# Row fetches by SyncE alone, and index lists read in place, in the gather rounds of a graph network

## What is computed

```python
def _round(x, w, b, gamma, beta, src, dst, etype):
    h = jax.nn.relu(_bn(x, gamma, beta))
    h = jnp.einsum('nd,od->no', h, w) + b
    msg = h.reshape(N, T, D)[src, etype]
    return jax.ops.segment_sum(msg, dst, num_segments=N)
# x = layernorm(x + round2(round1(x)) + x)
# then: h = x @ W_in; W_ij = (ssp(f_ij @ Wf1 + bf1) @ Wf2 + bf2) * cutoff
# out = segment_sum(h[src] * W_ij, dst); x = layernorm(x + ssp(out @ Wo1 + bo1) @ Wo2 + bo2)
```

## Time and profile before

| | |
|---|---|
| median of 3 runs | 8460.24 us (8458.51 to 8467.58) |
| the profiled execution, first to last instruction | 8446.8 us |
| TensorE's mean granted clock in it | 0.707 of full speed |
| TensorE matmul busy | 4102.0 us (49%) |
| DVE busy | 3975.2 us (47%) |
| ACT busy | 1426.6 us (17%) |
| Pool busy | 4532.3 us (54%) |
| first and last start of a table gather, round 0 | 212.9 and 2778.1 us |
| the same, round 1 | 2959.0 and 5539.9 us |
| table gathers in both rounds | 2886 |
| first row fetch of SP in round 0 | 234.0 us |

### The profile page before, as it was taken

The page is one execution under the profiler, slowest core; times in us unless marked ns, Lnnn a source line. Parts: engine busy times, 40 slices in busy tenths (PEclk is TensorE's granted clock), DMA queues, the critical chain, the costliest instruction groups (busy, mean ns, idle before and its releaser), DMA issues. The chain is left out here.

```text
span 8446.8 us, 99538 instructions
## 1 busy us (share of the span) xinstructions
PE 4102.0 (49%) x22648; PEld 3353.5 (40%) x22648; DVE 3975.2 (47%) x7789; ACT 1426.6 (17%) x3513; POOL 4532.3 (54%) x4709
## 2 busy tenths in 40 slices
PE   7342232331023734322232104466667888888888
PEld 3232222221022423222222103345555776777777
DVE  4553333331023567555555205643333555555568
ACT  3000000000000200000000000034444444444423
POOL 4665555564056566555555306656666555555533
PEclk8666666665566766666666556776777899888989
DMA  7111111111012511111111102222223555555567
GB/s 268 46 45 41 42 42 43 42 43 30 7 46 58 190 48 44 42 42 42 43 41 41 27 11 77 79 88 91 93 91 121 171 172 171 170 169 169 171 218 233
DMA packets 467009, 761.62 MB, mean 90 GB/s; under 512 B 115518, under 2 KB 227712, under 8 KB 465698
## 3 DMA queue, kind: packets, MB, share of 16 engines
q1 hardware_dynamic: 310212, 436.97, 17.1%
q0 software_dynamic: 148032, 316.34, 13.1%
q10 hardware_dynamic: 8192, 2.11, 0.1%
HBM read 542.21 MB, written 212.75 MB: 89 GB/s over the span
## 5 line engine op out<-in xcount | busy, mean ns | idle before, releaser
L667 POOL DMA_INDIRECT edge_rows<-messages,idx_stage x1432 | 1368.4, 956 | 1059.3 <-DVE idx_stage L1043 648.2
L1756 PE MATMUL banks<-w_types,h_stage 128*128 128x512 f32 x320 | 321.5, 1107 | 1864.1 <-issue 1153.5
L667 POOL DMA_INDIRECT buf_a<-messages,idx_stage x727 | 695.7, 957 | 715.8 <-DVE idx_stage L1043 487.8
L728 POOL DMA_INDIRECT sorted_rows<-edge_rows,idx_stage x784 | 760.4, 970 | 543.3 <-DVE edge_rows L1576 329.8
L728 POOL DMA_INDIRECT sorted_rows<-buf_a,idx_stage x784 | 760.2, 970 | 538.4 <-DVE buf_a L1576 305.0
L667 POOL DMA_INDIRECT buf_x<-messages,idx_stage x727 | 696.5, 958 | 647.5 <-DVE idx_stage L1043 418.8
L1951 PE MATMUL banks<-work,buf_a 128*128 128x128 f32 x5640 | 839.6, 312 | 144.3 <-issue 98.7
L1951 PEld LDWEIGHTS banks<-work,buf_a 128*128 128x128 f32 x5640 | 798.1, 225 | 196.9 <-issue 187.2
L1756 PEld LDWEIGHTS banks<-w_types,h_stage 128*128 128x128 f32 x320 | 77.1, 299 | 1901.5 <-issue 1175.4
L1998 PE MATMUL banks<-wf,work 128*128 128x128 f32 x3136 | 616.1, 333 | 188.3 <-issue 180.3
L1998 PEld LDWEIGHTS banks<-wf,work 128*128 128x128 f32 x3136 | 487.9, 226 | 363.2 <-issue 362.5
(11 more groups left out here) (222 smaller groups left out, 7592.6 us busy)
## 6 DMA issues: line engine op xcount, KB each, us to landing
buf_a<-sorted_rows SPq DMA_DIRECT2D x705, 288.0 KB
messages<-work SPq DMA_DIRECT2D x196, 320.0 KB
buf_a<-dst_rows SPq DMA_DIRECT2D x198, 256.0 KB
first_batch<-messages SPq DMA_DIRECT2D x2048, 0.5 KB
buf_x<-messages ACTq DMA_DIRECT2D x2048, 0.5 KB
buf_x<-messages SPq DMA_DIRECT2D x2048, 0.5 KB
buf_a<-messages ACTq DMA_DIRECT2D x2048, 0.5 KB
buf_a<-messages SPq DMA_DIRECT2D x2048, 0.5 KB
```

Of the source, the lines that this page charges most:

```text
L667: nc.gpsimd.indirect_dma_start(gathered[p][h][:, t, :], None, source, bass.IndirectOffsetOnAxis(ap=idx_stage[:, h, t:t + 1], axis=0),).the ...
L728: nc.gpsimd.indirect_dma_start(sorted_rows, bass.IndirectOffsetOnAxis(ap=idx_stage[:, 2 * u + h, t:t + 1], axis=0), msg_halves[2 * u + h][ ...
L1756: nc.tensor.matmul(ps_raw[:, 0:WIDE], h_stage[:, t % 2, :], w_types[p][:, 0:WIDE], start=True, stop=True)
```

## The change

The groups that are fetched row by row go from ten to six (three batches, 24 tiles a round instead of 40), and SP issues all of them, each batch whole, in `fetch_batches`; nothing is fetched late, and ACT fetches nothing. `idx_stage`, `s_idx` and `stage_indices` are gone: Pool gives its DMAs the columns of `msg_idx` (in the convolution of `places`) themselves. In the gather pass Pool waits for `s_agg`, TensorE's sums of the half four earlier. Before the second memset it waits for `msg_idx`. TensorE waits for the one-hot matrix once a half instead of once a group. The wide path is reordered.

```diff
-FETCHED = ((112, 0), (114, 0), (132, 0), (134, 0), (148, 0), (150, 0), (176, 0), (178, 0), (184, 0), (186, 0))
+FETCHED = ((112, 0), (114, 0), (148, 0), (150, 0), (184, 0), (186, 0))
 BATCHES = len(FETCHED) // 2
-SP_BATCHES, ACT_BATCHES = (0, 2, 4), (1, 3)
-FETCH_HALF = (None, 2, 3, 5, 6)
-ACT_FIRST_RAW, ACT_UNITS = RAW_TWICE, 4
-LATE_FIRST, LATE_UNITS = {4: 80, 3: 104}, 3
+FETCH_HALF = (None, 3, 6)
...
             def fetch_batches(p):
                 sp.wait_ge(s_setup, FETCH_LINKS)
-                for i in SP_BATCHES:
+                for i in range(BATCHES):
                     if i:
                         sp.wait_ge(s_raw_agg, raw_summed(p, i))
                     if p:
                         sp.wait_ge(s_acc[0], SUMS + 2 * (FETCHED[2 * i + 1][0] - 2 * RAW_ITERS[0] + 1))
-                    for e in late_units(i, 0) if i in LATE_FIRST else range(P):
-                        fetch_rows(nc.sync, mybir.EngineType.SP, p, i, e)
+                    for e in range(P):
+                        fetch_rows(p, i, e)
...
                     fetch_batches(0)
                     for m in range(CHUNKS):
                         store_nodes(TURNED + m, m, y_row_stage)
-                        fetch_late(0, m + 1)
...
                 load_x(m + 1)
-                fetch_late(1, m)
                 store_chunk(m)
...
                 for half in range(2 * RAW_ITERS[p], 2 * ITERS):
                     h = half % GATHER_SLOTS
-                    pool.wait_ge(s_idx[p], half + (1 - 2 * RAW_ITERS[p]))
+                    if half >= 2 * RAW_ITERS[p] + GATHER_SLOTS:
+                        pool.wait_ge(s_agg[p], half + (1 - 2 * RAW_ITERS[p] - GATHER_SLOTS))
...
                             gathered[p][h][:, t, :], None, source,
-                            bass.IndirectOffsetOnAxis(ap=idx_stage[:, h, t:t + 1], axis=0),
+                            bass.IndirectOffsetOnAxis(ap=msg_idx[:, half * HALF_TILES + t:half * HALF_TILES + t + 1], axis=0),
...
             gather_raw(0)
+            pool.wait_ge(s_setup, RANGE_LINKS + 2)
             nc.gpsimd.memset(buf_a[:, 6 * WIDE:NBUF], 0.0).then_inc(s_clear, 1)
...
                 for h in range(2):
-                    pool.wait_ge(s_idx[2], r * 2 + (h + 1))
                     pool.wait_ge(s_tagged, r * 2 + (h + 1))
...
-                                sorted_rows, bass.IndirectOffsetOnAxis(ap=idx_stage[:, 2 * u + h, t:t + 1], axis=0),
+                                sorted_rows, bass.IndirectOffsetOnAxis(ap=places[:, column:column + 1], axis=0),
...
-                    if t >= ACT_FIRST_RAW:
-                        fetch_some(rnd, ACT_UNITS)
-                fetch_some(rnd, P + LATE_FIRST[ACT_BATCHES[-1]] - (RAW_TILES - ACT_FIRST_RAW) * ACT_UNITS)
...
-                    fetch_some(0, LATE_UNITS)
...
                 deviation(m)
-                fetch_some(1, LATE_UNITS)
...
-                stage_indices(p, k + GATHER_SLOTS, 2 * u + h)
...
-                    stage_indices(2, k, 2 * u + h)
```

More of the change, by code:

```diff
@@ L22 @@
-import itertools
 import numpy as np
@@ L389, in raw_summed, with fetch_rows @@
             return RAW_BEFORE[p] // HALF_TILES + FETCH_HALF[i] + 2
[L391 to L395, removed]
+        def fetch_rows(p, i, e):
             rows = table[p].rearrange("(o n) d -> o (n d)", o=1).bitcast(u8)
             at = nc.values_load_multi_w_load_instructions(
-                fetch_at[e:e + 1, i, :, :].rearrange("p j t -> p (j t)"), engines=[kind], min_val=0,
+                fetch_at[e:e + 1, i, :, :].rearrange("p j t -> p (j t)"), engines=[mybir.EngineType.SP], min_val=0,
                 max_val=(N * T - 1) * ROW_BYTES, skip_runtime_bounds_check_because="a source times the types plus a type, in bytes")[1]
@@ L401, in fetch_rows @@
             for t in range(HALF_TILES):
-                engine.dma_start(into[:, t * ROW_BYTES:(t + 1) * ROW_BYTES], rows[:, ds(at[t], ROW_BYTES)]
+                nc.sync.dma_start(into[:, t * ROW_BYTES:(t + 1) * ROW_BYTES], rows[:, ds(at[t], ROW_BYTES)]
                                  ).then_inc(s_fetched[i], 16)
@@ L1795, in aggregate, with rows_in @@
                 rows_in_slot = gathered[p][slot]
-                hot, rows_of = hots[h if beyond else slot], []
+                hot = hots[h if beyond else slot]
+                def rows_in(j):
+                    if j and closing:
+                        return rows_in_slot[:, GROUP_TILES:HALF_TILES, :]
+                    if isinstance(r2, int) and (r * 2 + h, j) in FETCHED:
+                        batch, part = divmod(FETCHED.index((r * 2 + h, j)), 2)
+                        pe.wait_ge(s_fetched[batch], (p + 1) * FETCH_INC)
+                        return fetched[p][batch].rearrange("p (t n) -> p t n", n=P)[
+                            :, part * GROUP_TILES:(part + 1) * GROUP_TILES, :]
+                    pe.wait_ge(s_gather[slot][j], gathers(p, slot, j, r2, r2 if passed is None else passed))
+                    return rows_in_slot[:, j * GROUP_TILES:(j + 1) * GROUP_TILES, :]
+                if beyond:
+                    sum_beyond(p, rows_in, r * 2 + h)
                 for j in range(2):
@@ L1800, in aggregate @@
                     if j and closing:
-                        rows_of.append(rows_in_slot[:, GROUP_TILES:HALF_TILES, :])
                         continue
[L1803 to L1813, removed]
+                    rows_in_group = rows_in(j)
                     if j == 0:
-                        pe.wait_ge(s_acc[p], g + (2, 6)[p])
+                        pe.wait_ge(s_onehot[p], r2 * 4 + (2 * u + h + 1 - 2 * RAW_ITERS[p]))
+                        pe.wait_ge(s_acc[p], r2 * 8 + (4 * u + 2 * h - 4 * RAW_ITERS[p] + (2, 6)[p]))
                     tiles = LAST_TILES if closing else GROUP_TILES
@@ L1961, in beyond_block @@
                     tile = slice(t * P, (t + 1) * P)
-                    last = nc.tensor.matmul(ps_h[j][:, tile], x_onehot[:, 0, tile], x_h, start=opening, stop=False)
+                    last = nc.tensor.matmul(ps_h[j][:, tile], x_onehot[:, 0, tile], x_h, start=False, stop=False)
                 last.then_inc(s_xagg[2], 1)
@@ L1977, in convolution_step @@
                         if beyond:
[L1978 to L1980 removed]
+                            nc.tensor.matmul(ps_h[j], ones_d[0:1, :], zero_col[0:1, :].broadcast_to([1, WIDE]), start=True, stop=False)
+                            with pe.Fori(0, BLOCKS) as b:
+                                beyond_block(k, j, b)
                         for t in range(GROUP_TILES):
@@ L1984, in convolution_step @@
                             last = nc.tensor.matmul(ps_h[j][:, tile], spread[:, h, edges], h_win[:, h, j, :],
-                                                    start=not beyond, stop=True)
+                                                    start=not beyond, stop=not beyond or t == GROUP_TILES - 1)
                         last.then_inc(s_hexp, 1)
```

39 lines of the change are left out of this document (10 added, 29 removed).

## The result

The changed kernel takes 8695.84 us (median of 4 runs, 8676.12 to 8711.81) against 8463.91 us (4 runs) for the kernel before: 232 us slower, and by the runs' means 1.0267 times as long (95% interval 1.0242 to 1.0292). The forecast was 8800. The profiled execution's span is 8674.3 us, 227.5 us above the one before, so the profile holds nearly the whole difference.

What follows compares the result with a forecast made beforehand. SP's row fetches bound each round, at half 148 and at the first stores or loads behind them. Terms 30 + 328 - 20 = +338 us on the 8446.8 span, plus 13.4, gave 8798, say 8800; range 8610 to 8990.

Steps and rivals of the forecast that it cites:

- (b): Third batch: 384 more rows ahead of the first stores (round 0) or `load_x(1)` (round 1), 164 us each, +328 us.
- (a): Gather rounds until half 148's fetched rows: longer streams (gapless Pool gathers) slow SP's rows, +15 a round, +30 us (bounds -16, +254).
- (c): Tails, each round's end behind the fetches: eight more gathers, shorter Pool pauses, together about -20 us (bounds +20 and -132).
- (d): Start: memset waits for msg_idx, first gather some 7 us later; Pool's 70 us wait before half 152 covers it, 0.
- (e): ACT issues 4,096 rows less; raw tiles end ahead of SP's wait at half 148; worth counted in (a), one-hot wait 0.
- (f): Gathers reading the index lists in place: same 955 ns each, 0.
- (g): Third phase: 196 index copies of 165 ns leave DVE, no Pool scatter wait is on them: 0 (bound -32).
- Streams run together: Rival (22%): Pool's gather streams grow to four halves or more, SP falls to 1.8 us a row; 8964 us.
- Faster: Rival (9%): ACT's rows slow SP's; alone SP keeps 0.427 us a row beside Pool, nothing waits for batch three; 7594 us.
- The block is hidden: Rival (4%): first store or load behind the third batch is needed later than read, (b) is 0; 8470 us.

Runs made afterwards that it cites:

- late_back: Changed kernel, but 48 of the last batch's 128 partitions fetched behind the stores and loads, as before: 0.9867 of the kernel before, 8351 us on 8464.
- one_batch_2: Changed kernel with only the first batch (groups 112 and 114) fetched, other groups gathered by Pool, in a slow set: 7515.32 us, 0.8873 of the kernel before.
- before_again: The kernel before, unchanged, run again for its profile, in a quick set: 6277.59 us (one run).

## Why the prediction was right, and where it was off

**What bounds the kernel** was read rightly: SP's rows, twice a round. The strongest evidence is that taking the third batch away, and then the second, made the kernel 643 and then, in another set, 954 us faster than the one before, while Pool did more. In a quick set the same kernel before is not bound by SP.

**(b), the block:** +328 forecast; +158.4 and +162.8 in the profile, 321.2 together, 0.418 us a row against the 0.427 used. late_back gives the same from the other side (0.040).

**(a), up to half 148:** forecast +30, measured -43.1 and -22.8, -65.9, beyond the bound of -16 that I gave it. This is the main miss, and it has three steps. I let streams lengthen once ACT was out (+15 a round). They did not (from 19.9 to 19.6 us in the mean between 700 and 1400 us, though 3 of the 30 came to 30 us). The pauses fell from 5.9 to 2.9 us, more than the 0.8 us a pause which I gave to the copy, since ACT's rows had held TensorE. And I charged each microsecond of pause that goes with a row per 0.427 us; counted by start, a row in a pause took 0.63 us in the kernel before and 0.78 in the changed one. By the same reading too few rows of the 198.5 us were left for the streams, so that 1.28 us a row beside a stream was too slow: over round 0's streams up to half 148 it was 1.03 before and 1.00 after. In the kernel before the two errors cancel (2026 for 2034.3), so that it could not show them; with fewer pauses they do not. Short pauses were worth less to SP than I thought, and streams more. That the total still lay in my range is due to (b), which is the larger term and was right. Pool came to half 152 at 1832.6 and stood 174.2 us, in which SP ran at its full pace.

**(c), the tails:** forecast -20; -13.8 and -14.9, -28.7. **(d), the start:** forecast 0 with cover; the memset's wait moved the first gather by 10.3 us and SP's first row from 234.0 to 241.8, and as SP is the bound its own later start has no cover. I named Pool's waiting as the cover and overlooked that SP waits at the same table: the step failed by some 8 to 10 us. **(e), ACT:** "what that is worth is in (a)" had the wrong sign there, as shown. **(f)** held, 955 ns. That the copies do not slow the gathers held too, though the median in the earlier trace rows could not show it: 176 gathers of the kernel before ran beside a copy and took 954 ns in the mean, the others 957. **(g):** forecast 0, measured -7.2. In sum -65.9 + 321.2 - 28.7 + 10.3 - 7.2 - 2.2 = 227.5 against the 338 forecast; 96 of the 110 us between them are (a)'s.

**The signs named:** the third batch ran from 2002.7 to 2483.0 (said: 2050 to 2530), the pauses were 406.4 at half 159 (380) and 428.8 at half 154 (430), the short ones 3.0 (3.2). SP's last row for half 148 came at 2001.5, just inside the 2000 that would have called (a) wrong, and only because the first gather came 10.3 us later.

**The rivals.** *Streams run together* did not come where SP still has rows: a mean of 19.6 us between 700 and 1400 us, and up to half 148 of round 0 7 of 74 streams over 28 us (2 of 69 in the kernel before). Behind SP's last row of round 0 it did come. From 2490 us to the end of the round Pool has nine streams, eight of them of 40 us, where the kernel before has 17 of 20.1 in the mean. It costs nothing there, since SP has no row to issue, and is part of (c). Pool's waits from 2490 to 2890 us:

```profile
POOL buf_x L649 <- remote: 45.4, 9, 5.2
```

*Faster* needed SP under 0.69 us a row; it took 0.73 (241.8 to 2483.0 for 3,072). ACT was not what slowed it: inside the streams between 700 and 1400 us SP's rows took 1.01 us before and 0.97 after (19.9 us for 19.6 rows, 19.6 for 20.3). By the Trainium skill, "DMA: Bandwidth & Descriptors", section "Issuing engines are not separate DMA queues", the issuers' DMAs run on the same 16 engines, which alone would have let SP's pace rise by what ACT left; the trace gives it a twentieth. In the quick sets SP does have the 0.43 us of that rival, and the change still gains nothing, because there Pool never waited for SP in the kernel before either. *The block is hidden* fell with late_back.

## What to carry to other kernels

Price work that is moved in a queue by what stands behind it: 384 of SP's 3,072 rows cost 12 to 17 us a round behind the stores and 160 ahead of them. Two removals that each look like a gain may not add; a wait that is shortened shows the next holder, here ACT, so test them apart and together. And see a kernel in more than one set of runs before tuning its overlap: one batch is 11% faster than the kernel before in a slow set and 1% slower in a quick one.

## What was not expected of the hardware

Of five sets of runs, three had the kernel before at 8464, 8588 and 8469 us, two at 6279 and 6273. Neither the gathers' own records tell them apart (955 and 952 ns, and one_batch_2 has 952 in a slow set), nor TensorE's mean granted clock (0.707 and 0.721), nor the set's chip number. What differs is what runs beside the gathers.

In the slow sets an increment that TensorE makes some way into a stream is seen some 3 us after Pool stops: the sums that end at 990.8 in the changed kernel, 6.6 us into a stream, reach DVE at 1006.99. In a quick set it is seen while Pool gathers (before_again):

```profile
435.39 2.08 PE L1819 MATMUL banks<-x_onehot,buf_x 128*128 128x128 f32 x8 [3.31 <-DMA buf_x<-messages,idx_stage]
...
437.60 0.29 DVE L1166 TENSOR_TENSOR buf_a<-buf_a,banks 128x128 f32 x1 [4.04 <-PE banks L1819]
...
437.82 0.95 POOL L667 DMA_INDIRECT edge_rows<-messages,idx_stage  x1 [0.30 <-issue]
```

SP's rows take some 0.45 us each in a stream's first 3 us and some 1.9 to 2.3 between its 10th and 20th in the first set (both kernels, both rounds, up to half 148), and 0.427 us throughout in the quick one. In the third phase too the kernel before takes 2906.9 us in the one and 2324.5 in the other (3951.2 to 6275.7). No run here shows what in the chip, the machine or its setting makes the two kinds.
